# A recommendation tower on one core: the low parts of three of the fifteen looked-up tables are made by GpSimd instead of VectorE

## What is computed

```python
e = jnp.stack([tbl_0[ids[:, 0]], ..., tbl_25[ids[:, 25]]], axis=1)      # 512 x 26 x 128
combined = jnp.concatenate([dense_features[:, None, :], e], axis=1)     # 27 vectors
interactions = jnp.einsum('bnd,bmd->bnm', combined, combined)
z = jnp.concatenate([dense_features, interactions[:, _TRIU_I, _TRIU_J]], axis=1)
h = jnp.concatenate([z, r_dense_features], axis=1)
h = jnp.maximum(h @ W_top1 + b_top1, 0.0)        # 607 x 512
h = jnp.maximum(h @ W_top2 + b_top2, 0.0)        # 512 x 256
y = h @ W_top3                                   # 256 x 1
```

## Time and profile before

| | |
|---|---|
| time, median of 3 runs | 121.43 us |
| the profiled execution: its time / its span | 120.86 us / 118.8 us |
| TensorE busy | 110.5 us, 93% |
| VectorE busy | 72.8 us, 61% |
| ScalarE busy | 59.2 us, 50% |
| GpSimd busy | 52.5 us, 44% |
| chain that ended last: TensorE / VectorE / issue | 83% / 9% / 3% |
| mean granted TensorE clock | 0.971 |

### The profile page before, as it was taken

The page is one execution under the profiler, slowest core; times in us unless marked ns, Lnnn a source line. Parts: engine busy times, 40 slices in busy tenths (PEclk is TensorE's granted clock), DMA queues, the critical chain, the costliest instruction groups (busy, mean ns, idle before and its releaser), DMA issues.

```text
span 118.8 us, 3660 instructions
## 1 busy us (share of the span) xinstructions
PE 110.5 (93%) x1573; PEld 90.3 (76%) x1573; DVE 72.8 (61%) x160; ACT 59.2 (50%) x111; POOL 52.5 (44%) x52
## 2 busy tenths in 40 slices
PE   5999999979999999999997999766999999999991
PEld 2377578848888888888885899654799999999970
DVE  3799999999899997999399700070072053044020
ACT  3729967994497776790999050301020211113441
POOL 2777778778877777778777700000000000000000
PEclk9999999999999999999999999985599999999999
DMA  4899999999996799649942200000000000000000
GB/s 87 283 303 282 279 256 258 246 273 247 268 263 138 199 258 257 159 92 337 397 145 50 61 22 6 6 0 6 6 6 6 6 0 6 6 6 0 0 0 1
DMA packets 6044, 15.48 MB, mean 130 GB/s; under 512 B 1655, under 2 KB 2427, under 8 KB 5902
## 3 DMA queue, kind: packets, MB, share of 16 engines
q1 hardware_dynamic: 4452, 12.20, 36.9%
q0 software_dynamic: 1408, 2.89, 9.9%
q10 hardware_dynamic: 170, 0.18, 0.7%
HBM read 15.26 MB, written 0.00 MB: 129 GB/s over the span
## 4 chain that ended last, share of the span: by engine, by line
PE 83%; DVE 9%; issue 3%; DMA 2%; ACT 1%; DVEq 0%
PE ps_a L355 46%; PE ps_gram L392 10%; DVE onehot L544 6%; PE ps_rows L426 5%; PE ps_h L440 5%; PE ps_a L426 5%; PE ps_rows L370 5%; DMA idrow<-ids_by_table 2%; PE ps_rows L416 2%; PE ps_z L403 2%; PE ps_a L453 2%; DVE part_sb L553 2%; PE ps_a L416 1%; DVE table_sb L571 1%; PE ps_h L466 1%
## 5 line engine op out<-in xcount | busy, mean ns | idle before, releaser
L355 PE MATMUL ps_a<-onehot,part_sb 125*128 125x512 f32 (+1 forms) x272 | 63.6, 386 | 1.9 <-issue 1.7
L327 POOL DMA_INDIRECT rows_sb<-tbl,ids_sb x44 | 51.9, 1179 | 15.3 <-issue 13.1
L355 PEld LDWEIGHTS ps_a<-onehot,part_sb 125*128 125x128 f32 x272 | 47.7, 188 | 13.7 <-issue 4.0
L544 DVE TENSOR_SCALAR onehot<-idrow,row_id 125x512 fp32r<-125x512 int16 (+1 forms) x78 | 42.2, 602 | 2.6 <-DMA idrow<-ids_by_table 1.5
L553 DVE TENSOR_TENSOR part_sb<-table_sb,part_sb 125x512 fp32r<-125x512 f32 (+1 forms) x30 | 20.6, 716 | 2.0 <-ACT part_sb L610 2.0
L571 DVE STREAM_TRANSPOSE table_sb<-ps_gram 128x864 f32<-128x864 f32 x4 | 4.3, 1083 | 26.6 <-PE ps_gram L392 26.6
L631 ACT COPY xt<-ps_a 128x512 f32<-128x512 f32 (+1 forms) x16 | 10.0, 628 | 19.0 <-PE ps_a L355 11.9
L610 ACT CAST part_sb<-table_sb 125x1024 fp32r<-125x1024 f32 (+2 forms) x16 | 16.8, 1056 | 2.7 <-DMA table_sb<-tbl 2.7
L392 PE MATMUL ps_gram<-xt 128*27 128x27 f32 x1024 | 13.1, 201 | 2.8 <-issue 2.1
L392 PEld LDWEIGHTS ps_gram<-xt 128*27 128x27 f32 x1024 | 11.1, 114 | 5.6 <-issue 4.2
L638 ACT COPY xt<-ps_rows 128x128 f32<-128x128 f32 (+2 forms) x32 | 8.2, 340 | 5.6 <-PE ps_rows L370 5.4
(11 more groups left out here) (33 smaller groups left out, 44.4 us busy)
## 6 DMA issues: line engine op xcount, KB each, us to landing
table_sb<-tbl SPq DMA_DIRECT2D x11, 448.0 KB
table_sb<-tbl SPq DMA_DIRECT2D x4, 560.0 KB
idrow<-ids_by_table SPq DMA_DIRECT2D x5, 256.0 KB
w_sb<-w SPq DMA_DIRECT2D x1, 1280.0 KB
rows_sb<-tbl,ids_sb POOLq DMA_INDIRECT x44
table_sb<-tbl SPq DMA_DIRECT2D x10, 52.0 KB
idrow<-ids_by_table SPq DMA_DIRECT2D x4, 128.0 KB
w_sb<-w SPq DMA_DIRECT2D x1, 512.0 KB
```

The lines of the kernel that those rows point to most:

```text
L327: pool.indirect_dma_start(rows_sb[:, t % ROWS_RING, GATHERED.index(f), :], None, tables[f], bass.IndirectOffsetOnAxis(ids_sb[:, t, f:f + 1 ...
L355: last = pe.matmul(ps_a[:, (h + piece) % 2, a:b], parts_sb[part][:, w, c * D:(c + 1) * D], unit_onehot(u, c)[:, member, a:b], start=(part ...
L544: dve.tensor_scalar(unit_onehot(u, c), idrow[0:VP, w, 0:n, :], row_id[0:VP, first + c:first + c + 1], None, ALU.is_equal).then_inc(onehot_ ...
```

## The change

A new table `LOW_BY_GPSIMD = {0: 2, 5: 16, 10: 31}` names tables 0, 5 and 10. VectorE no longer makes their low parts. GpSimd does, with the same subtraction, each table right before the gather whose number stands there (counted from 0). Since the low parts now come from two engines, GpSimd counts its own on a new semaphore, and whoever waited for a low part waits on the one that belongs to its table: TensorE before a low quarter, SyncE before it loads table h+4.

```diff
+LOW_BY_GPSIMD = {0: 2, 5: 16, 10: 31}
...
+    _places = {_c: [(h, half) for h, half in halves if h not in LOW_BY_GPSIMD] for _c, halves in _places.items()}
...
-LOW_AT_END = [(h, half) for h in _owed for half in range(2)]
+LOW_AT_END = [(h, half) for h in _owed for half in range(2) if h not in LOW_BY_GPSIMD]
...
+def low_number(h, half):
+
+    same = [x for x in range(h) if (x in LOW_BY_GPSIMD) == (h in LOW_BY_GPSIMD)]
+    return 2 * len(same) + 1 + half
...
+        def low_ready(h):
+
+            return low_by_gpsimd_ready if h in LOW_BY_GPSIMD else part_ready[LOW]
...
-                    sp.wait_ge(part_ready[LOW], 2 * (h - TABLE_RING + 1))
+                    sp.wait_ge(low_ready(h - TABLE_RING), low_number(h - TABLE_RING, 1))
...
+            def make_low(h):
+                s, w, middle = h % TABLE_RING, h % WORK_RING, CHUNKS[h] // 2 * D
+                if h >= WORK_RING:
+                    pool.wait_ge(lookup_done, h - WORK_RING + 1)
+                for half, columns in enumerate((slice(0, middle), slice(middle, CHUNKS[h] * D))):
+                    pool.wait_ge(part_ready[HIGH], rounded(h, half))
+                    pool.tensor_tensor(parts_sb[LOW][:, w, columns], table_sb[0:VP, s, columns],
+                                       parts_sb[HIGH][:, w, columns].bitcast(F32), ALU.subtract) \
+                        .then_inc(low_by_gpsimd_ready, 1)
...
+                    for h, gather in LOW_BY_GPSIMD.items():
+                        if gather == issued:
+                            make_low(h)
...
-                            pe.wait_ge(part_ready[LOW], 2 * h + 1 + half)
+                            pe.wait_ge(low_ready(h), low_number(h, half))
...
-            dve.wait_ge(part_ready[LOW], 2 * NOH)
+            dve.wait_ge(part_ready[LOW], 2 * (NOH - len(LOW_BY_GPSIMD)))
+            dve.wait_ge(low_by_gpsimd_ready, 2 * len(LOW_BY_GPSIMD))
```

More of the change, by code:

```diff
@@ L217, in build @@
         part_ready = [sem(f"part{i}_ready") for i in PARTS]
+        low_by_gpsimd_ready = sem("low_by_gpsimd_ready")
         lookup_done = sem("lookup_done")
```

## The result

The changed kernel takes 126.8 us (median of 4 executions, 126.4 to 128.6); the kernel before, with one more execution, 121.4. The ratio is 1.043, with an interval of 1.034 to 1.053: slower, near the 126.0 us that were forecast. Some executions of a kernel take over 1.5% longer than its fastest, and every ratio here compares the medians of the others. The profiled execution took 126.98 us, with a span of 125.2.

The account below looks back on a forecast made before the run. TensorE's back-to-back lookup matmuls were taken to bound the kernel from 13.02 us on. Lateness at table 10, a vanished wait and the clock, 4.35 - 0.70 + 1.5 = 5.15 us, on 120.86 gave 126.0 us; range 121.3 to 130.0.

Parts of the forecast that it names:

- The price of a subtraction: One low-part subtraction on GpSimd, taken at 1.2 us, by the nearest row, the mean gather.
- The bounds of the unknown price: GpSimd's subtraction at 0.68 us puts low(10,0) at 52.5, total 121.4 us; at 2.26 us, at 60, total 132.
- Table 0: At start-up, VectorE relieved of table 0's pair starts its next one-hots earlier: a gain of 0.4 us at 13.02.
- GpSimd's queue: Subtractions shift gathers and stand behind them: low(10,0) ready at 55.6, TensorE 4.35 us behind, waiting 1.5 and 3.2 us.
- What gives back: Late in the lookups, TensorE's wait at 64.38 us should go: -0.70 us.
- The wait at 64 + 4: TensorE's 0.70 us wait for low(13,0), at 64.38 before the change, expected to be gone once everything comes 4 us later.
- the stated condition: The 0.70 us wait hangs on ScalarE's 2.87 us hold-up before copying lookup 10; if held up again, it stays.
- The clock: Behind the 3.2 us standstill the granted clock may halve for 6 us, losing 3 us or none; middle taken, +1.5 us.
- The blocking of engines: Rival: GpSimd's subtractions and VectorE's one-hots hold each other up, +2 to +3 us before low(10,0), total 129 us; chance 0.18.
- The queue that is not late: Rival: at 1.32 us a gather step instead of 1.49, low(10) comes just in time, total 120.5 us; chance 0.19.
- The argument against blocking: The gather at 21.04 beside VectorE's one-hots took 1.01 us, no more than others; but gathers need not read likewise.

Follow-up runs that it names:

- after again: The changed kernel unaltered, run a second time for its trace and time, also called the repeat: ratio to the kernel before 1.045.
- tables 5 and 10: The changed kernel with table 0's low part left to VectorE, GpSimd making those of tables 5 and 10: ratio to the kernel before 1.016.
- low halves earlier: The kernel before, nothing on GpSimd, VectorE making the first low half of tables 4, 7, 10 and 13 before the fifth one-hot: ratio 0.992.
- table 10 two gathers earlier: The changed kernel with table 10's subtractions before gather 29 instead of 31: ratio to the kernel before 1.038.
- table 5 alone: The kernel before, with GpSimd making the low part of table 5 only, at gather 16: ratio 1.024.
- spare subtractions: The kernel before, VectorE making all low parts, plus two GpSimd subtractions on spare tiles at each of three places, nobody waiting for them: ratio 1.054.
- The fills: The kernel before, plus two GpSimd fills of a spare tile, written and not read, at each of three places: 122.35 us beside 121.8.
- table 10 alone: The kernel before, with GpSimd making the low part of table 10 only, at gather 31: ratio 1.022, not decided by its time.
- marks: The kernel before, no GpSimd subtraction, but two extra gathers at each of three places, each followed by a small fill that TensorE waits for: ratio 1.065.
- all three earlier: The changed kernel with table 5's subtractions two gathers earlier (14) and table 10's three earlier (28): ratio to the kernel before 1.076.
- the single-table runs: The kernel before, with GpSimd making the low part of only table 0 (124.3 to 128.8 us), 5 (ratio 1.024) or 10 (1.022).

## Why the prediction was right, and where it was not

**The price of a subtraction.** Taken at 1.2 us; it is 1.26, and at table 0, where VectorE came in between, 1.4. The Trainium skill (GPSIMD Engine Reference, section 3.1) gives the ratio 1.96, by which I had estimated 1.3 us; the 1.26 us of this trace agree with it. The bounds of the unknown price were summed wrong: five subtractions lead to low(10,0), so at 0.68 us it would come at 53.0 and at 2.26 us at 60.9, not at 52.5 and 60.

**Table 0.** Wrong in sign. A gain of 0.4 us at 13.02 was forecast, a loss of 1.0 us came. The step that failed is "VectorE starts the next unit's one-hots at 6.45 instead of 7.65": it started them at 7.61. GpSimd's pair held the last one-hot of unit [0] until 7.69 and the first of the next unit until 9.39, and the eleven one-hots took 7.69 us, where seven at 0.41 and four at 0.675 us a step are 5.6. low(1,0) came at 11.29, forecast 9.84, before 10.23. Table 1's rounding was later too (9.31 instead of 8.79) but done by 10.4, before VectorE wanted it. How large the loss is at group 0 varies with the execution: 1.0 us (after less before), 0.3 us (after again less tables 5 and 10, of one batch).

**GpSimd's queue.** Right. Shift at gather 3, forecast 2.0, measured 1.75; gather 15 ended at 29.91, forecast 29.4. low(10,0) was forecast for 55.6, and came at 55.78. TensorE's lag at that point was 55.83 - 51.25 = 4.58 us, forecast 4.35. That this moment doesn't depend on what was lost earlier is borne out: TensorE came 1.3 us later than forecast to table 5 (30.5 instead of 29.2), and waited there for 0.79 us instead of 1.5, and for 2.67 instead of 3.2 at table 10, as it was later by itself.

**What gives back.** Right: from group 6 to group 9 the lag falls from 58.69 - 53.83 = 4.86 us to 71.76 - 67.94 = 3.82. The wait at 64 + 4 is gone. The late end of lookup 10 did not come in this execution, which was the stated condition. So this gain is the late end's absence and not the change's doing.

**The clock.** The forecast term of 1.5 us was the middle between nothing and 3 us, and neither the middle nor the 3 came. In the profiled execution the clock stayed at 1.00 behind the wait, and the term measured nothing; in the repeat the same wait of 2.67 us was followed by 0.50, and cost 1.6 us. Behind 4.74 us it was 0.50 too, and cost about 2. So it is a term that some executions pay, at about half the 3 us.

**Behind the lookups.** Not in the sum at all: the part from group 9 to the end took 53.4 us instead of 50.9. TensorE stood still for 1.55 and 1.72 us in it (1.04 and 1.09 before), and the half clock fell on busy stretches (92 to 95 us). These 2.6 us filled the place of the missing clock term, and that the total came out so near the forecast is partly luck. The twelve traces of the experiments have 51.4 to 57.9 us there, also those whose lookups were not touched by GpSimd (low halves earlier: 53.4). In that run TensorE stood still there for 4.0 us with no releaser in the trace, after the change for 3.8, before for 2.1. So I take it for the spread of executions, in which the profiled one of before was a short one, and not for an effect of the change; that was not tested by itself.

**The rivals.** The blocking of engines was given 0.18 with 129 us. Its mechanism is real, and falls mostly on the other engine: GpSimd was held for 0.3 us at table 0 and not at the other two, VectorE for 2 to 3 us at each. That it did not add to the time at tables 5 and 10 after the change is because TensorE was waiting there for the late queue anyway, so VectorE had room. Take the lateness away (table 10 two gathers earlier, or table 5 alone), and the shut-out comes forth as the next wait: 1.55 and 0.8 us. The queue that is not late was wrong: steps between gathers stayed near 1.5 us. (Its 1.49 us a step was itself misread; 42.3 us for 28 steps are 1.51.) The argument against blocking, that gathers beside one-hots take 1.01 us, was no argument, as was said there. One-hots beside gathers keep their 0.41 and 0.675 us a step, beside GpSimd's subtractions they do not. Whether VectorE holds up gathers stays open: most take 1.0 to 1.2 us beside it, a few 1.8 to 2.65 (after, the one at 18.97).

## What to carry to other kernels

An instruction that is moved to a queue with room comes as late as what stands ahead of it there: cost the moment at which its result is ready, not its duration. Before taking VectorE's work to GpSimd, ask what VectorE does in that time; here six subtractions of 0.68 us were saved and 2 to 3 us were lost at each of three places. And where an engine waits for another, look at that engine's order first: putting a low half three one-hots earlier took away the wait at lookup 4, which the move to GpSimd left at 0.74 us.

## What the runs showed of the hardware

- **A subtraction on GpSimd shuts VectorE out.** In 18 of the 23 pairs in these traces, which took 2.50 to 2.56 us, VectorE ended nothing between the two subtractions, and the instruction that it had in hand, if any, ended only behind both: 3.65 us (after), 3.34 us for a one-hot of 0.48 (after, at 29.41), 3.58, 3.61 and 3.40 us (spare subtractions). Its recorded start lies up to 0.6 us ahead of the pair (53.92 and 54.50). The other five pairs took 2.8 to 3.3 us, and there VectorE finished one instruction between the two. The Trainium skill (SBUF — State Buffer, Who interferes with whom) has the rule: two SBUF inputs on VectorE against GpSimd's reads, a two-port mode against any. The fills agree with it, 1.1 us on the one-hots and nothing on the low parts, if the one-hots run in such a mode, which no run here shows by itself. By that rule whoever comes first has the port for one instruction; here GpSimd mostly kept it for two in a row.
- **The clock behind a standstill.** With the same 2.67 us of standstill the granted clock stayed at 1.00 (2.4 GHz) in one execution and fell to 0.50 (1.2 GHz) in the other.
- **A late end of a lookup.** In 7 of the 14 profiled executions ScalarE, VectorE or GpSimd, whichever waited for a lookup's end, got it late, mostly by 2.4 us or more and nearly at the same moment, while TensorE went on until it needed them: before at lookup 10 (done at 53.99, copied at 56.39), table 10 alone at lookup 8 (ScalarE 48.69, VectorE 48.76), marks (ScalarE 49.51, GpSimd 49.74). No record shows what delays it. One of them made TensorE stand still for 5.33 us (all three earlier, until 82.25). It may be why the times of the single-table runs decide so little; that was not traced execution by execution.
